# Spacing the work that shares two PSUM banks in an attention kernel, and putting TensorE's waits on its weight loads

## The reference

```python
qkv = x @ c_attn.T + b;  q, k, v = split(qkv)          # 16 heads of 64
w   = softmax(q * 64**-0.5 @ k.T + causal_bias)
x   = layernorm(x + (w @ v) @ c_proj.T + b_proj)
x   = layernorm(x + gelu(x @ w1 + b1) @ w2 + b2)
```

## Time and profile before

| | us |
|---|---|
| median of 3 runs | 2384.45 (2384.28 to 2605.83) |
| the profiled execution | 2386.43 |
| its span on core 3, the slowest | 2384.9 |
| spans of the eight cores | 2361.6 to 2384.9 |
| first exp to last exp on core 3 | 35.1 to 1328.0 |
| TensorE busy, share of the span | 2147.8 (90%) |
| ScalarE busy | 1359.0 (57%) |
| VectorE busy | 753.1 (32%) |

### The profile page before, as it was taken

How to read it: one execution, slowest core, us unless ns; L and a number is a source line. 1 busy time by engine, 2 the same in 40 slices (tenths; PEclk the granted TensorE clock), 3 DMA queues, 4 the chain that set the end, 5 groups by cost and what they waited for, 6 DMA issues and landing times.

```text
span 2384.9 us, 68463 instructions; the slowest of 8 cores (2361.6 to 2384.9 us)
## 1 busy us (share of the span) xinstructions
PE 2147.8 (90%) x30242; PEld 1376.1 (58%) x30242; DVE 753.1 (32%) x1925; ACT 1359.0 (57%) x1666; POOL 218.0 (9%) x181
## 2 busy tenths in 40 slices
PE   7998888898988989888768899999999999999997
PEld 3444655655556556555545566666666666666665
DVE  3433434343333343343312132222233322222221
ACT  1677788898998989989879422222222222222222
POOL 2000000000000000000110221111111111111110
PEclk8999999999999999999879999999999999999999
DMA  9500100001000000000491511001111111111000
GB/s 141 90 15 7 29 9 14 14 7 29 9 8 19 10 20 10 7 12 9 104 164 30 110 45 36 27 27 45 45 45 45 45 45 45 45 45 45 18 5 32
DMA packets 52638, 89.95 MB, mean 38 GB/s; under 512 B 3200, under 2 KB 35968, under 8 KB 51328
## 3 DMA queue, kind: packets, MB, share of 16 engines
q0 software_dynamic: 16784, 33.56, 9.1%
q1 hardware_dynamic: 35568, 52.00, 6.5%
HBM read 93.94 MB, written 25.17 MB: 50 GB/s over the span
## 4 chain that ended last, share of the span: by engine, by line
PE 69%; ACT 18%; DVE 8%; issue 2%; DMA 2%; POOL 0%; POOLq 0%; SPq 0%; DVEq 0%
ACT work L552 18%; PE ps L929 18%; PE ps L911 18%; PE ps L604 9%; PE ps L405 8%; PE ps L535 6%; PE ps L753 4%; DVE qkv L435 2%; DVE work L946 2%; PE ps L365 1%; PE ps L272 1%; DVE stat L456 1%; PE ps L406 1%; DVE qkv L483 1%; PE ps L642 1%
## 5 line engine op out<-in xcount | busy, mean ns | idle before, releaser
L552 ACT ACTIVATE work<-ps,cb 128x1024 bf16<-128x1024 f32 (+3 forms) x1152 | 1112.6, 1065 | 186.7 <-PE ps L535 179.9
L919 ACT ACTIVATE work<-ps,b_s 128x256 bf16<-128x256 f32 x512 | 243.8, 476 | 790.7 <-PE ps L911 790.7
L604 PEld LDWEIGHTS ps<-qkv,work 64*128 64x128 bf16 x16896 | 480.0, 96 | 331.7 <-issue 246.8
L604 PE MATMUL ps<-qkv,work 64*128 64x65 bf16 x16896 | 609.9, 193 | 29.9 <-issue 13.5
L929 PE MATMUL ps<-qkv,work 128*128 128x512 bf16 x2048 | 526.2, 379 | 21.6 <-DVE work L946 20.9
L911 PE MATMUL ps<-work,xT 128*128 128x256 bf16 x4096 | 532.8, 273 | 0.7 <-issue 0.7
L535 PE MATMUL ps<-qkv 64*128 64x512 bf16 (+3 forms) x2304 | 443.1, 370 | 71.9 <-ACT work L552 64.4
L911 PEld LDWEIGHTS ps<-work,xT 128*128 128x128 bf16 x4096 | 401.8, 98 | 157.2 <-issue 1.4
L929 PEld LDWEIGHTS ps<-qkv,work 128*128 128x128 bf16 x2048 | 198.1, 98 | 208.8 <-issue 29.6
L405 PE MATMUL ps<-xT,work 64*128 64x512 bf16 x896 | 270.2, 380 | 13.4 <-DVE stat L456 13.4
L406 PE MATMUL ps<-xT,work 64*128 64x512 bf16 x896 | 270.6, 381 | 0.0
(11 more groups left out here) (58 smaller groups left out, 1110.9 us busy)
## 6 DMA issues: line engine op xcount, KB each, us to landing
work<-x SPq DMA_DIRECT2D x16, 1024.0 KB, 5.1
out<-work SPq DMA_DIRECT2D x16, 1024.0 KB, 4.0
attn_s<-work SPq DMA_DIRECT2D x64, 128.0 KB, 1.8
xT<-w POOLq DMA_DIRECT2D x8, 1024.0 KB, 14.1
work<-attn_s SPq DMA_DIRECT2D x16, 512.0 KB, 6.4
qkv<-w POOLq DMA_DIRECT2D x16, 512.0 KB, 8.1
xT<-xb POOLq DMA_DIRECT2D x7, 1024.0 KB, 47.1
work<-wqk POOLq DMA_DIRECT2D x7, 512.0 KB, 5.9
```

The lines of the kernel that those rows point to most:

```text
L552: lambda: sc.activation(pb, ps, AF.Exp, bias=cb[:, 8 * p + g : 8 * p + g + 1], scale=0.125),
L604: r = t.matmul(bank(6 + h)[:, 65 * c : 65 * c + 65], pbuf[i % NP][rows, 512 * h + 128 * c : 512 * h + 128 * c + 128], w[rows, o : o + 65], ...
L919: lambda: sc.activation(hbuf[ui % 4], bank(4 + ui % 2)[:, 0:TB], AF.Gelu, bias=b1[:, hc : hc + 1]),
```

## The change

Six things are changed, all in the attention.

- `GAP` is gone. Instead the first step of a group (`paired`) and each norm are `heads`: none is taken before unit `ready`, which is two units after the last step of the group or the norm before it, and one unit after a turn.
- A unit takes at most about three full passes (`spent < 3.0`), or six half-wide ones.
- The credit added in a unit is what is left in the queue, shared over the units that are left until `until` (142 after the start of a pair).
- Turns come before the queue's steps in a unit, not behind them, and only from unit `ready` on.
- `attN` and `rden` have three buffers, not two; the work area grows by 512 columns.
- TensorE's lane is fused too: the last wait of each instruction is carried by its weight load. `warm` returns its first matmul as well, so that it can carry one.

```diff
-        self.fuse = name in ("act", "dve")
+        self.fuse = name in ("act", "dve", "pe")
...
+    heads = set()
+    now = [0]
+    ready = [0]
...
+    def paired(cost, step):
+        out = [(cost, step(n)) for n in range(16)]
+        heads.add(out[0][1])
+        return out
...
                     gb_open[0] = gb_open[1] = False
+                    ready[0] = now[0] + 2
                 return n == 7
             return go
-        return [(1.0 + (GAP if n == 0 else 0.0), step(n)) for n in range(16)]
+        return paired(1.0, step)
...
             bound(p, g)
-        return [(3.0 + GAP, go)]
+            ready[0] = now[0] + 2
+        heads.add(go)
+        return [(3.0, go)]
...
-        return [(0.5 + (GAP if n == 0 else 0.0), step(n)) for n in range(16)]
+        return paired(0.5, step)
...
-    attN_free = [None] * 2
+    attN_free = [None] * 3
...
     def run_fill(all_=False):
-        while fill and (all_ or credit[0] >= fill[0][0]):
+
+        spent = 0.0
+        while fill and (all_ or (credit[0] >= fill[0][0] and spent < 3.0)):
+            if fill[0][1] in heads and now[0] < ready[0] and not all_:
+                break
             c, go = fill.popleft()
             credit[0] -= c
+            spent += c
...
-                rate[0] = sum(c for c, _ in fill) / (4 * g + 3)
+                until[0] = i + 4 * g + 3
...
-                rate[0] = sum(c for c, _ in fill) / 138.0
+                until[0] = i + 142
...
-                rate[0] = 0.9
+                until[0] = i + 56
...
-        credit[0] += rate[0]
+        now[0] = i
+        while turns and i - turns[0][0] >= 5 and not gb_open[0] and not gb_open[1] and i >= ready[0]:
+            turn_block(*turns.popleft()[1:])
+            order[1] = True
+            ready[0] = i + 1
+        credit[0] += (sum(c for c, _ in fill) - credit[0]) / max(1, until[0] - i)
         run_fill()
...
-        while turns and i - turns[0][0] >= 5 and not gb_open[0] and not gb_open[1]:
-            turn_block(*turns.popleft()[1:])
-            order[1] = True
```

More of the change, by code:

```diff
@@ L23 @@
 NP = 7
-GAP = 3.0
 NB = S // TB
@@ L124, in build_nc @@
     cexp = sb("cexp", 4, F32)
-    rden = sb("rden", 16, F32)
+    rden = sb("rden", 32, F32)
     bvb = sb("bvb", D, F32)
@@ L129, in build_nc @@
     bigB = sb("qkv", 2 * HB, BF16)
-    bigC = sb("work", 27 * 1024, BF16)
+    bigC = sb("work", 27 * 1024 + 512, BF16)
     xT = bigA
@@ L146, in cut @@
         c_at[0] += n
-        assert c_at[0] <= 27 * 1024, c_at[0]
+        assert c_at[0] <= 27 * 1024 + 512, c_at[0]
         return a.bitcast(F32) if dt == F32 else a
@@ L152, in build_nc @@
     pbuf = [cut(1024) for _ in range(NP)]
-    attN = [cut(512) for _ in range(2)]
+    attN = [cut(512) for _ in range(3)]
     attC = [cut(512) for _ in range(4)]
@@ L226, in warm @@
     def warm():
+        a = None
         for _ in range(30):
             r = t.matmul(bank(6), ones, sq[0], start=True, stop=True)
-        return r
+            a = a or r
+        return a, r
     pe.put(warm, t_warm, t_ones)
@@ L621, in divide @@
     def divide(p, g, tok):
-        n = (NG * p + g) % 2
+        n = (NG * p + g) % 3
+        assert all((NG * q + h) % 3 != n for _, q, h in turns)
         acc = PS[:, 3072:4096].rearrange("p (h c) -> p h c", h=2)[:, :, 0:260].rearrange(
@@ L641, in go @@
             for c in range(4):
-                r = t.transpose(pb[:, 128 * c : 128 * c + 128], attN[k % 2][:, 128 * c : 128 * c + 128], idb)
+                r = t.transpose(pb[:, 128 * c : 128 * c + 128], attN[k % 3][:, 128 * c : 128 * c + 128], idb)
                 a = a or r
             return a, r
-        attN_free[k % 2] = tok = pe.put(go, done, gb_free[u], ld_idb)
+        attN_free[k % 3] = tok = pe.put(go, done, gb_free[u], ld_idb)
         gb_free[u] = ev = dve.put(lambda: v.tensor_copy(attC[k % 4], pb[:, 0:512]), tok, attC_free[k % 4])
@@ L813, in build_nc @@
     credit = [0.0]
-    rate = [0.0]
+    until = [0]
     def run_fill(all_=False):
-        while fill and (all_ or credit[0] >= fill[0][0]):
+        spent = 0.0
+        while fill and (all_ or (credit[0] >= fill[0][0] and spent < 3.0)):
+            if fill[0][1] in heads and now[0] < ready[0] and not all_:
+                break
             c, go = fill.popleft()
             credit[0] -= c
+            spent += c
             order[1] = True
@@ L888, in build_nc @@
     end_pe = t_pv[NU - 1]
-    end_turn = attN_free[(NPAIR * NG - 1) % 2]
+    end_turn = attN_free[(NPAIR * NG - 1) % 3]
     block_mem[2] = (end_pe, end_turn)
```

## The result

| | before | after |
|---|---|---|
| time, us | 2384.45 | 2305.03 (2301.99 to 2409.63, 4 runs) |
| ratio, both run on one chip | 1 | 0.9663, 95% from 0.9635 to 0.9691 |
| the profiled execution, us | 2386.43 | 2304.15 |
| its slowest core's span, us | 2384.9 (core 3) | 2302.6 (core 2) |

The kernel is 3.4% faster, about 80 us, where 54 were forecast. Executions in which one die ran at a lower clock, among them the one profiled in e11 (where only cores 0 to 3 are read), are left out of the ratios and of the time of e11; the other times are medians of all executions, at most 1.3 us above those without them.

A forecast was written before the change was run, and what follows sets the result against it. ScalarE's exps, paused by late TensorE, were taken to bound attention, TensorE the feed-forward layer. Turns -46, heads -14, norms +15, pair 1 +13, packing +6, waits -28 made -54 us: 2330 us, own range 2312 to 2350, wide 2296 to 2370.

The forecast's parts named there:

- The waits: TensorE's waits carried by weight loads: 0.075 us in each of 380 late units, -28 us, bounds 0 and -40.
- The clock of pair 7: Pair 7, without passes, shows a granted clock of 0.86 and was said not to change.
- Turns: Pairs 0 to 6: turns no longer right behind a closing step, so those ScalarE pauses go, -46 us.
- Heads: Starts of groups, all now two units behind a norm or group: 17.6 us of waits go, -14 us.
- Norms: Norms two units behind their group wait for VectorE's squares: 25 such against 6 before, +15 us.
- The end of pair 1: Pair 1's queue doesn't fit: 34 steps done at its end with ScalarE idle, +13 us.
- Packing: Pairs 2 to 5: units with three passes grow from 20 to 28 each, about 1 us a pair, +6 us.
- (a): Rival: fused waits give nothing, placement does as forecast, 2358 us; chance 0.18.
- (b): Rival: norms' second wait absorbed, end of pair 1 costs half, waits give 40 us: 2300 us; chance 0.15.
- (c): Rival: feed-forward weight loads with a wait inside lose their lead, +102 us, slower than before at 2460; chance 0.05.
- (d): Rival: units with few passes at turnovers slow the clock in pairs 2 to 5, +24 us, 2354 us; chance 0.12.
- The other signs: Pair lengths: pair 0 shorter by 15 us, pairs 2 to 5 by 5 to 9 each, pair 1 by less.

The follow-up runs named there:

- e11: The kernel before with one more 512-column matmul, its result unread, in most units of blocks 1 to 5 of pair 7: 2394.16 us, ratio 1.0042.
- e1: The kernel before with only TensorE's waits fused into its weight loads, placement old: 2323.06 us, ratio 0.9741.
- e4: The changed kernel with only the wait ahead of the second half of the values a separate instruction again: 2345.01 us.
- e10: The changed kernel with only the wait in front of the scores a separate instruction again: 2324.68 us.
- e2: The changed kernel with all TensorE waits as separate instructions again, so the placement alone: 2367.20 us, ratio 0.9926.
- e3: The changed kernel with turns placed behind the queue's steps again, free of `ready`: 2331.85 us.
- e8: The changed kernel with norms three units behind their group, not two, in pairs 2 to 6: 2308.79 us.
- e6: The changed kernel with groups of half-wide passes in pair 1 blocking the next head for one unit, not two: 2297.16 us.
- e7: The changed kernel without the cap of three passes a unit: 2294.69 us.
- e5: The changed kernel run again, unedited: 2305.95 us.

## Why the prediction was right and wrong

**Direction and range.** The direction held, and so did the wide range of 2296 to 2370, which took in the rivals. The forecast of 2330 was 25 us too high, and its own range, 2312 to 2350, was missed: the placement gave 18 us for 26, the waits 62 for 28. The waits' miss was made smaller by the placement's, which went the other way; that is luck.

**The waits: the step that failed is the count.** The price per wait was about right: 0.075 us was forecast; 0.059 and 0.062 (the two weight loads) and 0.086 (values matmul behind the scores) were measured. I counted 380 units in which it would matter. 62 us divided by 0.086 would be some 720. The places, by e1 and the table: pair 0 11.0 (forecast 144 x 0.075 = 10.8, right), pair 1 10.4 (forecast 4.5), pairs 2 to 5 6 each (forecast 1.9), pair 6 4.0 (forecast 1.9), pair 7 7.5 (forecast 3.8). From the exps' starts, some 20 of the 23 us in pairs 2 to 5 can be sorted: 8.6 lie in units with a turn, 2.5 at norms, 2.3 at heads, about 7 in the short units at the ends of blocks. So two things were missed. The upper bound of 40 was thought of "if the waits behind evictions gain as well", and they did: 0.24 us became 0.05. And a unit isn't either late or in time. The reading that fits is that 0.06 to 0.09 us given to every unit lets TensorE go into the next burst, turn or row of short units further ahead of ScalarE; it is argued from where the time went, no run shows it by itself. e4 shows the half's wait alone is worth 39 us, 2.3 to 3.0 in each of pairs 2 to 5, and e10 the scores' wait 19. In the new order these two make 58 of the 61.

**The clock of pair 7.** The prediction said that it doesn't change. Low time per core went from 33 to 54 us down to 7 to 20, and in each experiment in which one wait stands apart it came back: 34 to 51 in e4, 24 to 44 in e10, 48 to 61 in e2. About half of what e10 loses is in this pair. The fused waits in the old order leave 20 to 38 (e1), so the 7 to 20 take the new order as well. That the separate waits lower the clock there is shown; by what, isn't. In e11 added matmuls left 27 to 40. The Trainium skill (TensorE: Matmul & The Clock Gate, A second HAM failure mode: psum-queue depth-cycling) describes a kernel whose brief, frequent idle times between groups of matmuls made the clock go back and forth. Pair 7 agrees with it so far as shorter idle times went with less low time: the mean idle time between TensorE's matmuls there, of those above 0.05 us and as the median of the cores, is 0.34, 0.37, 0.41, 0.43, 0.44 and 0.50 us in the changed kernel, e1, e10, the kernel before, e4 and e2, with 10, 27, 38, 41, 43 and 51 us at 1.2 GHz. e11 doesn't fit (0.50 with 28, in fewer idle times), and which of the two follows the other isn't shown; why the new order alone (e2) makes it worse than before, by 8.0 us, stays open too.

**Turns.** The mechanism was right, the waits of L642 went from 34.3 to 0.4 us. The term was mis-sized: e3 gives 27 for the forecast 46 (in pair 0 2.3 for 6). The forecast price of a pause was that of the kernel with separate waits; with fused ones a turn behind a closing step pauses ScalarE 1.17 us, not 1.85. The 0.68 between is booked under the waits; 0.19 of it is the release of the transposes, the rest isn't split up. And a part of each pause seems to be recovered by the units behind it: in e3 six turns in each of pairs 2 to 5 stand right behind a closing step, by the order in the trace, and cost some 4.0 us, 0.7 each, a little under the 0.8 to 1.85 read from the rows.

**Heads.** The waits of 17.6 us ahead of groups are 3.4. What this gave in time (14 forecast) no run shows by itself.

**Norms.** 25 norms at two units were forecast for pairs 1 to 6, and the trace has 25 there (4 in pair 1, 5 in each of pairs 2 to 5, 1 in pair 6; 3 more in pair 0). Their waits in pairs 1 to 6 rose from 4.4 us in 6 to 13.2 in 15. Delaying them gains nothing inside the pairs: e8 takes those waits away and pays as much in fuller units. But the dearest ones, forecast at 1.8 us, are the last of each pair, and e8 leaves them (1.46 us of pause for 1.58). These some 6 us seem to come from letting the queue run to the pair's last units; no run tries to get them back. What the whole term (+15) is worth no run gives. That these units lose 0.74 us each was read from pair 1 before the change; with fused waits it is 0.58.

**The end of pair 1.** 34 steps left over, and a pause of 12 to 14 us were forecast; it is 16.4. The pair as a whole got shorter all the same by 6.9, because the fused waits took 10.4 (e1). As a term, e6 shows 8.6 us and e7 12.4 to be had there (e7 with the cap gone as well).

**Packing.** The cap was priced through the fuller units of pairs 2 to 5 (20 before by the prediction; the order in the trace has 17, two of them with 3.5 passes). It is the cap's absence that costs there (1.4 us each, e7), and its presence in pairs 0 and 1 (1.9 to 3.5, and 12.4) that costs most: "0 to +6, inside the range" for pair 0 was right.

**The rivals.** (a), fused waits that give nothing, is out by e1. (b), more than counted, is the one that came nearest (2300 against 2305), for one of its three reasons, the waits, and that beyond its 40 us; the end of pair 1 cost more than forecast, not half. (c) is out: in the feed-forward layer the weight load keeps its lead, as in the earlier trace rows.

```profile
1803.37 0.97 PEld L933 LDWEIGHTS ps<-work,xT 128*128 128x128 bf16 x8
1803.58 1.04 PE L933 MATMUL ps<-work,xT 128*128 128x256 bf16 x8
```

0.21 us ahead, with its wait inside; the rest behind the last exp is 1054.8 in e1 and 1057.5 in e2 and in the changed kernel (before 1054.0), so what differs by 3 us there doesn't go with the waits; the changed kernel unedited had 1055.8 in another execution (e5). (d), holes that slow the clock in pairs 2 to 5, didn't come: the granted clock in pair 4 is 1.00 after 0.99, and the time at 1.2 GHz in pairs 2 to 5, as medians of the cores, fell from 3 to 7 us a pair to 0 to 2.

**The other signs.** Pair 0 got shorter by 10.2 us where 15 were forecast, pairs 2 to 5 by 9.3 to 10.4 where it was 5 to 9.

## What to carry to other kernels

A wait written as an instruction of its own in front of a TensorE instruction costs little each time, but where two engines run a tenth of a microsecond apart it counted in more units than those in which a pause was seen. Price it with two bounds, the units in which the engine is late and all units: here 28 us (380 units) and 99 (1152 times 0.086), and 62 were measured. And put the wait on the weight load first. When work that shares banks is spaced, count first whether the spaced sequence fits into its stretch; a rule that holds in four pairs left 34 steps over in the fifth. A cap on bursts belongs only where the other engine sets the time, not where TensorE has the most to do.

## What the hardware showed that was not expected

- A weight load that carries its wait starts 0.051 to 0.060 us behind its release, one with the wait ahead of it 0.113 to 0.119; the matmul behind it gains 0.086 (medians of e4 and the changed kernel; e2 and e10 for the exp). At one turn behind an eviction it was 0.24 before against 0.05 in e1. Together 62 us of 2384 (e1).
- A carried wait that is met already doesn't keep the weight load from running ahead: 0.21 us with and without, in the feed-forward layer.
- The granted clock of a stretch without passes followed TensorE's waits: pair 7 spent 33 to 54 us of some 151 at 1.2 GHz before, 20 to 38 with fused waits in the old order (e1), 7 to 20 of 140 after, and with the new order 24 to 61 whenever one or all of the waits stood apart.
